# Moving the sums and squares of two layer norms from VectorE's batch statistics to ScalarE's accumulator output

## The reference

```
def _ln(x, w, b, eps=1e-05):
    m = x.mean(-1, keepdims=True)
    v = ((x - m) ** 2).mean(-1, keepdims=True)
    return (x - m) / jnp.sqrt(v + eps) * w + b
...
xa = _ln(x, ln1_w, ln1_b)            # "recurrent" norm, on the MLP's result
... token shift, mixes, projections, decay w, scan s = a + w * s, group norm og ...
x1 = x + og * g @ Wo.T
xc = _ln(x1, ln2_w, ln2_b)           # "channel" norm, on the recurrent part's result
sx2 = jnp.concatenate([state[:, 0:1] - xc[:, :1], xc[:, :-1] - xc[:, 1:]], axis=1)
rr = jax.nn.sigmoid((xc + sx2 * ffn_maa_r) @ Wfr.T)
kk = jnp.square(jax.nn.relu((xc + sx2 * ffn_maa_k) @ Wfk.T))
return x1 + rr * (kk @ Wfv.T)
```

## Time and profile before

| | |
|---|---|
| three timed runs | 1116.63, 1121.56, 1121.56 us, median 1121.56 |
| profiled execution | 1118.86 us, of which the span of the trace is 1117.1 |
| busy over the span | PE 1061.3 us (95%), DVE 916.1 (82%), ACT 702.6 (63%), POOL 608.1 (54%) |
| steady steps | from about 540 to 910 us |
| steps with the first channel runs, then the list behind step 15 | from about 936 and about 1020 us |
| granted TensorE clock | 0.989 of full speed |

### The profile page before, as it was taken

The page is one execution under the profiler, slowest core; times in us unless marked ns, Lnnn a source line. Parts: engine busy times, 40 slices in busy tenths (PEclk is TensorE's granted clock), DMA queues, the critical chain, the costliest instruction groups (busy, mean ns, idle before and its releaser), DMA issues.

```text
span 1117.1 us, 34410 instructions
## 1 busy us (share of the span) xinstructions
PE 1061.3 (95%) x12992; PEld 883.5 (79%) x12992; DVE 916.1 (82%) x1662; ACT 702.6 (63%) x1606; POOL 608.1 (54%) x535
## 2 busy tenths in 40 slices
PE   5999999999999998999999999999999998788898
PEld 4888988888889887777787877777777776566687
DVE  5997777888777776228999999999999999999753
ACT  5678878777777775465556555456555455544574
POOL 4787887877887885024443454443454443444233
PEclk9999999999999998999999999999999999998999
DMA  8500000011111110013333331233331233304011
GB/s 328 174 4 2 0 0 2 3 41 41 41 48 38 38 47 3 1 28 68 79 83 86 85 70 40 64 81 84 84 76 40 56 82 86 85 10 114 20 38 57
DMA packets 39867, 65.01 MB, mean 58 GB/s; under 512 B 4384, under 2 KB 26208, under 8 KB 39392
## 3 DMA queue, kind: packets, MB, share of 16 engines
q1 hardware_dynamic: 39776, 63.75, 21.4%
HBM read 55.35 MB, written 8.39 MB: 57 GB/s over the span
## 4 chain that ended last, share of the span: by engine, by line
PE 60%; DVE 27%; issue 7%; ACT 3%; DVEq 1%; DMA 1%; SPq 0%; POOL 0%; ACTq 0%; POOLq 0%
PE psum L353 9%; DVE shared L1788 9%; PE psum L267 5%; PE psum L999 5%; PE psum L336 5%; PE psum L1008 4%; PE psum L368 4%; PE psum L1089 4%; DVE shared L1774 4%; PE psum L297 4%; PE psum L280 3%; DVE late_mixed L1754 3%; PE psum L1270 2%; PE psum L310 2%; PE psum L1300 2%
## 5 line engine op out<-in xcount | busy, mean ns | idle before, releaser
L1788 DVE TENSOR_TENSOR_SCAN shared<-late_wT,shared 128x512 f32<-128x512 f32 x128 | 192.4, 1503 | 0.0
L232 POOL TENSOR_TENSOR shared<-shared,att_row_max 128x512 f32<-128x512 f32 x128 | 132.3, 1051 | 17.9 <-DVE att_row_max L564 17.9
L353 PE MATMUL psum<-shared 128*128 128x128 f32 x1024 | 126.6, 277 | 0.0
L453 ACT ACTIVATE shared<-shared 128x512 f32<-128x512 f32 x128 | 80.5, 631 | 67.7 <-POOL shared L232 67.6
L353 PEld LDWEIGHTS psum<-shared 128*128 128x128 f32 x1024 | 121.0, 194 | 0.3 <-ACT shared L462 0.2
L999 PE MATMUL psum<-late_glnT,w 128*128 128x256 f32 x512 | 119.5, 387 | 1.8 <-ACT late_glnT L1378 1.8
L1008 PE MATMUL psum<-w,late_hT 128*128 128x256 f32 x512 | 120.0, 383 | 1.0 <-ACT late_hT L1387 0.9
L564 DVE TENSOR_REDUCE att_row_max<-shared 128x8 f32<-128x512 f32 x128 | 86.9, 680 | 40.9 <-POOL shared L225 40.9
L903 POOL TENSOR_TENSOR shared<-shared,late_rT 128x512 f32<-128x512 f32 x32 | 40.7, 1273 | 140.6 <-DVE shared L1788 140.6
L894 POOL TENSOR_TENSOR late_xm<-late_mixed,late_xa 128x512 f32<-128x512 f32 x64 | 79.7, 1255 | 59.9 <-DVE late_mixed L1754 56.3
L999 PEld LDWEIGHTS psum<-late_glnT,w 128*128 128x128 f32 x512 | 95.8, 192 | 17.9 <-issue 2.8
(11 more groups left out here) (168 smaller groups left out, 2420.9 us busy)
## 6 DMA issues: line engine op xcount, KB each, us to landing
shared<-v_rows SPq DMA_DIRECT2D x64, 512.0 KB, 7.1
shared<-in_enc SPq DMA_DIRECT2D x64, 128.0 KB, 2.6
v_rows<-shared SPq DMA_DIRECT2D x64, 64.0 KB, 1.8
out<-x SPq DMA_DIRECT2D x16, 256.0 KB, 2.0
x<-in_x SPq DMA_DIRECT2D x7, 512.0 KB, 9.7
w<-in_w SPq DMA_DIRECT2D x2, 1024.0 KB, 16.9
shared<-in_cross_mask SPq DMA_DIRECT2D x1, 1024.0 KB, 11.4
shared<-in_w_qkv SPq DMA_DIRECT2D x1, 768.0 KB, 4.5
```

Source lines behind the costliest of these rows:

```text
L232: nc.gpsimd.tensor_tensor(zs, zs, peak.unsqueeze(2).to_broadcast([P, PAIRS, S]), ALU.subtract).then_inc(shifted, 1)
L353: last = nc.tensor.matmul(dst[:, half * P:(half + 1) * P], w[:, kb, c0 + half * P:c0 + (half + 1) * P], src[:, u % 2, kb, 0:P], start=(kb ...
L453: nc.scalar.activation(probs[:, u % 2, half * 4:(half + 1) * 4, :].rearrange("p r k -> p (r k)"), z[:, u % 2, half, :], ACT.Exp).then_inc( ...
L1788: nc.vector.tensor_tensor_scan(states, wT[:, u, half, :, :, :].rearrange("p j b t -> p (j b t)"), states, 0.0, ALU.mult, ALU.add).then_inc ...
```

## The change

The statistics of both norms go to ACT. For a run, `mlp_moments` is now: two Copy activations of the tile whose accumulator output is the row sum (the copied tile goes to `xn`, used as scratch), two small activations that scale the sums to -mean and to a shift, and two Square activations whose bias is the shift and whose accumulator output is the variance. `make_stats` is the same with one small activation, split in two functions, `out_means` and `out_variances`. DVE loses L1721 to L1731, L1857 and all of `ch_variances`; `ch_invert` reads the variances directly, and `ch_shifts` the sums.

```diff
+            def mlp_moments(g):
+                act.wait_ge(mlp_x, g + 1)
+                if later(g):
+                    act.wait_ge(xnT_ready, g)
+                act.nop(nofuse=True)
+                for c in range(CH):
+                    last = nc.scalar.activation(xn[:, c, :], core.x[:, ds(g * CH + c, C)], ACT.Copy,
+                                                accum_out=mlp_sum[:, c:c + 1])
+                last.then_inc(mlp_sum_ready, 1)
+                act.wait_ge(mlp_sum_ready, g + 1)
+                nc.scalar.activation(mlp_shift[:, :], mlp_sum[:, :], ACT.Copy, scale=-(C ** -1.5)).then_inc(mlp_mean_ready, 1)
+                nc.scalar.activation(neg_mean[:, :], mlp_sum[:, :], ACT.Copy, scale=-1.0 / C).then_inc(mlp_mean_ready, 1)
+                act.wait_ge(mlp_mean_ready, 2 * g + 2)
+                act.nop(nofuse=True)
+                for c in range(CH):
+                    last = nc.scalar.activation(xn[:, c, :], core.x[:, ds(g * CH + c, C)], ACT.Square, scale=C ** -0.5,
+                                                bias=mlp_shift[:, c:c + 1], accum_out=moments[:, CH + c:CH + c + 1])
+                last.then_inc(moments_ready, 1)
+            def out_means(r):
+                act.wait_ge(x_ready, r + 1)
+                act.wait_ge(xnT_ready, runs_by(r + 4))
...
+                nc.scalar.activation(out_shift[:, :], ch_mean[:, ds(r, CH)], ACT.Copy,
+                                     scale=-(C ** -1.5)).then_inc(out_mean_ready, 1)
+            def out_variances(r):
...
             def ch_invert(i):
-                act.wait_ge(norm_var, i + 1)
+                act.wait_ge(stats_ready, NORMS[i][1])
...
-                    for q in range(UPS):
-                        gelu(s + 3, q)
+                    gelu(s + 3, 0)
+                    gelu(s + 3, 1)
+                if there(s + 2):
+                    mlp_moments(s + 2)
+                if there(s + 3):
+                    gelu(s + 3, 2)
+                    gelu(s + 3, 3)
...
+                if there(s - 2) and not s_is(s, RUNS - 1):
+                    out_means(s - 2)
                 if there(s - 1) and not s_is(s, RUNS - 1):
                     square(s - 1)
...
+                if there(s - 2) and not s_is(s, RUNS - 1):
+                    out_variances(s - 2)
                 if not s_is(s, RUNS - 1):
                     nc.scalar.preload_act_table_set("natural_log_exp_and_others")
...
             ch_square(EARLY + 1, 1)
+            make_stats(RUNS - 3)
             square(RUNS - 1)
...
             ch_tanh(EARLY + 3, 1)
+            make_stats(RUNS - 2)
             channel(EARLY + 3, 1)
             ch_copy_in(EARLY + 6, 0)
+            make_stats(RUNS - 1)
             nc.scalar.preload_act_table_set("natural_log_exp_and_others")
             ch_invert(2)
```

More of the change, by code:

```diff
@@ new lines, in out_means @@
+            def out_means(r):
+                act.wait_ge(x_ready, r + 1)
+                act.wait_ge(xnT_ready, runs_by(r + 4))
+                act.nop(nofuse=True)
+                for c in range(CH):
+                    t = r * CH + c
+                    last = nc.scalar.activation(xn[:, c, :], core.x[:, ds(t, C)], ACT.Copy, accum_out=ch_mean[:, ds(t, 1)])
+                last.then_inc(out_sum_ready, 1)
+                act.wait_ge(out_sum_ready, r + 1)
+                act.nop(nofuse=True)
+                nc.scalar.activation(out_shift[:, :], ch_mean[:, ds(r, CH)], ACT.Copy,
+                                     scale=-(C ** -1.5)).then_inc(out_mean_ready, 1)
@@ new lines, in out_variances, with make_stats @@
+            def out_variances(r):
+                act.wait_ge(out_mean_ready, r + 1)
+                act.nop(nofuse=True)
+                for c in range(CH):
+                    t = r * CH + c
+                    nc.scalar.activation(xn[:, c, :], core.x[:, ds(t, C)], ACT.Square, scale=C ** -0.5,
+                                         bias=out_shift[:, c:c + 1], accum_out=ch_var[:, ds(t, 1)]).then_inc(stats_ready, 1)
+            def make_stats(r):
+                out_means(r)
+                out_variances(r)
@@ L1507, in ch_invert @@
                 part = slice(*NORMS[i])
-                act.wait_ge(norm_var, i + 1)
+                act.wait_ge(stats_ready, NORMS[i][1])
                 act.wait_ge(gxn_ready, RUNS)
-                nc.scalar.activation(core.norm_tmp[:, 0, part], core.norm_tmp[:, 2, part], ACT.Ln,
+                nc.scalar.activation(core.norm_tmp[:, 0, part], ch_var[:, part], ACT.Ln,
                                      bias=core.eps[:, :]).then_inc(norm_logged, 1)
@@ L1716, in mlp_residual @@
                 nc.vector.tensor_tensor(xs, mlp, xs, ALU.add).then_inc(mlp_x, 1)
-            def mlp_moments(g):
-                dve.wait_ge(mlp_x, g + 1)
-                for c in range(CH):
-                    last = nc.vector.bn_stats(run_stats[:, c, :], core.x[:, ds(g * CH + c, C)])
-                last.then_inc(run_stats_ready, 1)
-                dve.wait_ge(run_stats_ready, 2 * g + 1)
-                if later(g):
-                    dve.wait_ge(shift_ready, g)
-                dve.nop(nofuse=True)
-                for c in range(CH):
-                    last = nc.vector.bn_aggr(moments[:, c:c + CH + 1:CH], run_stats[:, c, :])
-                last.then_inc(run_stats_ready, 1)
-                dve.wait_ge(run_stats_ready, 2 * g + 2)
-                nc.vector.tensor_scalar(neg_mean[:, :], moments[:, 0:CH], -1.0, None, ALU.mult).then_inc(moments_ready, 1)
             def mixer_input(r):
@@ L1945, in body @@
                             ch_mix(early_run(s, 0), 0)
-                        if there(s + 2) and not s_is(s, -2):
-                            mlp_moments(s + 2)
                         if there(s - 2) and not early(s):
@@ L1952, in body @@
                         mix(s + 1, 1)
-                    if n == 3 and there(s - 2) and not s_is(s, RUNS - 1):
-                        make_stats(s - 2)
-                    if s_is(s, RUNS - 4) and n == 4:
-                        ch_variances(0)
                     if n == 4:
@@ L1981, in _ @@
             attention_residual(1, end)
-            mlp_moments(0)
             spreads(att.first_mlp)
@@ L1988, in _ @@
             add_heads(RUNS - 1, 1)
-            make_stats(RUNS - 3)
             sum_squares(RUNS - 2)
-            ch_variances(1)
             ch_mix(EARLY + 1, 1)
@@ L2001, in _ @@
             add_residual(RUNS - 2)
-            make_stats(RUNS - 2)
             ch_mix(EARLY + 4, 0)
@@ L2006, in _ @@
             add_residual(RUNS - 1)
-            make_stats(RUNS - 1)
-            ch_variances(2)
             ch_mix(EARLY + 5, 1)
```

40 lines of the change are left out of this document (11 added, 29 removed).

## The result

The changed kernel takes 1113.11 us (median of four runs, 1112.77 to 1115.22) beside 1121.1 of the kernel before; the recorded ratio of the runs is 0.9945, with a 95% interval from 0.9928 to 0.9962 (the two medians alone would give 0.9929). Run once more among later kernels it took 1115.20 (six runs), ratio 0.9953 [0.9936, 0.9969]. It is faster by about half a per cent, where I had forecast 1122 and no change. Its profiled execution took 1112.93 us with a span of 1111.1.

The account below looks back on a forecast made before the run. PE's own work was taken as the bound, 33.44 us a period, with DVE 0.07 above. Terms 0.6 + 1.3 - 1.4 - 1.4 - 0.7 - 1.5 + 2.8 + 2.8 = +2.5 us on 1119.6 gave 1122 us, range 1115.5 to 1129.5.

Parts of the forecast that it names:

- PE's own work is a floor of 33.44 us: Steady period: PE's work alone takes 33.44 us, DVE stands 0.07 above, so DVE's relief gives at most 0.07.
- +0.6: Steady steps 2 to 11: ACT's later `decay` starts the fifth mix 0.06 us later in each, +0.6 us.
- DVE would wait ahead of the fifth mix: Steady period: DVE, arriving 2.0 us earlier, waits at the fifth mix for `decay_expd`, so ACT's `decay` sets the period.
- The start: Step -2: `mlp_moments` at 3.05 us delays the gelus, and PE's `down` waits for the last one: +1.3 us.
- Step 12: Step 12: `ch_variances(0)` on DVE had pushed the mixes back; without it, -1.4 us.
- Step 13: Step 13: DVE reaches `ch_finish` 2.0 us earlier, but ACT can take the keys only some 1.4 earlier: -1.4 us.
- Step 14: Step 14: loses only DVE's statistics, -0.7 us.
- The list: Work behind the last step: less DVE work before the mixes -1.5 us; `make_stats(13)` and `make_stats(15)` in ACT's chain +2.8 each.
- r: What writing out the accumulator adds to an ACT activation: taken as 0.2 us, between nothing and 0.29.
- PE has room: Rival: matmuls close up once DVE is early, periods shrink towards 31.5 us, up to 20 us gained, 1100; chance 0.06.
- ACT sets the pace: Rival, slower: costlier accumulator writes or waits on ACT; +5.4 us at 0.29 a write, +9 (1128) at 0.4; chance 0.27.
- Only the end is faster: Rival: ACT's blocks at 1056 and 1084 hide, sum -3.1 us, 1119; chance 0.17 shared with a free accumulator.

Follow-up runs that it names:

- e1: Changed kernel with DVE also redoing its old batch statistics in the steps and at the start, into an unread scratch tile; 1120.94 us, ratio 1.0009.
- e2: Changed kernel with the two squares of `out_variances` done twice in each step, the extra pair into scratch; 1126.81 us, ratio 1.0078.
- e4: Kernel before with only `mlp_moments` moved to ACT, channel norms' statistics left on DVE; 1114.58 us, ratio 0.9955.
- e5: Kernel before with only the channel norms' statistics moved to ACT, `mlp_moments` left on DVE; 1117.25 us, ratio 0.9985.
- e11: Changed kernel run and traced once more, unaltered; 1115.20 us, ratio 0.9953.
- e12: Changed kernel with six unread matmuls in PE's wait ahead of the last block; 1115.04 us, ratio 0.9958.
- e2b: e2 with no accumulator output on the extra pair of squares; 1121.76 us, one run.
- e3: Changed kernel with the channel norms' last group of statistics, in the list at the end, given back to DVE; 1110.94 us, ratio 0.9925.
- e6: Changed kernel with `make_stats(13)` one place later in ACT's list and the statistics of `make_stats(15)` back on DVE; 1110.48 us, ratio 0.9916.
- e13: e6 with four unread matmuls in PE's wait ahead of `project_out(14)`; 1109.05 us, ratio 0.9904.
- e8: Changed kernel with ten unread matmuls in PE's wait ahead of the last block; 1116.47 us, ratio 0.9961.
- e9: Changed kernel with `make_stats(13)` moved as in e7, eight unread matmuls ahead of `project_out(15)` and ten ahead of the last block; 1115.85 us, ratio 0.9968.
- e7: Changed kernel with `make_stats(13)` one place later in ACT's list, behind a `ch_tanh`; 1113.10 us, ratio 0.9947.

## Why the prediction was wrong

**The step that failed is "PE's own work is a floor of 33.44 us ... Relief of DVE can give at most 0.07 us a period there".** The 33.44 us were not PE's own work. They held 0.17 us of waiting for DVE's last read of the states ahead of WrT (1.90 in place of 1.73 at 633.50), and the other periods up to 0.36; without it PE needs 33.24 us. The one period I read was also the shortest of the nine (33.43 to 33.60 us between L1026's starts). The chain laid it to PE, since the gap before the row is short (0.13 us at 700.48) and the rest of it stretches the row itself from 1.89 to 1.99. The wait of PEld in the earlier trace rows was that very wait, 0.4 us in each period, of which 0.27 reached the matmuls; I called it hidden "for the most part by the matmuls ahead" and didn't compare the row with others of its kind. With DVE's work gone the term is -2.78 and not +0.6; with it put back (e1) it is -0.57.

**That DVE would wait ahead of the fifth mix** was wrong: with the time it no longer loses it comes to the first mix before PE is ready, and waits there. Counted from where PE starts its `up` product of the period, before and after,

```profile
676.75 3.72 PE L999 MATMUL psum<-late_glnT,w 128*128 128x256 f32 x16
```

```profile
674.71 3.72 PE L1001 MATMUL psum<-late_glnT,w 128*128 128x256 f32 x16
```

ACT's copy of V comes at 13.52 us in both kernels (690.27 and 688.23). `decay` ends at 17.35 us (692.06) where it had ended at 17.11 (693.86): later by 0.24 and not by the 0.69 of the prediction, since `out_variances` takes 689.92 - 688.83 = 1.09 us where I had 1.41. The fifth mix then starts at 17.48 us, 0.31 earlier than before (694.54). The place was right all the same: one more microsecond there and ACT does set the pace (e2). The slack is 0.1 us.

**The start** was mis-sized: +1.3, measured +0.29. Of the difference 0.84 is `mlp_moments`, which moved the queue by 469.44 - 467.23 (the end of the second gelu pair) = 2.21 us where I had taken 3.05, and 0.14 that the last two gelu pairs ran without a gap (1.54 and not 2 x 0.84). e4 and e5 show that the 0.3 is `mlp_moments`'.

**Step 12** was right, -1.4 and -1.49, and for the reason given (e1 and e4 against e5). **Step 13**, -1.4 against -2.20: I let ACT's later work keep 0.6 of DVE's 2.0, and it kept nothing; PE's wait for `ch_finish` fell from 2.92 to 1.25 us. **Step 14**, -0.7 against -0.96, is right: with VectorE's statistics put back (e1) it is 35.58 us, in e4, where they never left VectorE, 35.65, and before 35.59, while e11 has 34.61 and the changed kernel 34.63.

**The list.** The -1.5 before the mixes was -2.2: from the account's -8.63 at the end of step 14 to 1042.42 - 1053.27 = -10.85 at the key product behind the mixes. From there to `project_out(14)` (1067.56 before, 1058.11 after) 1.40 us came back. That is `make_stats(13)`, in ACT's chain as said, for 2.3 us where I had 2.8, less 0.87 by which the product at 1053.27 was slower in the trace of before (2.88 us in its chain, 2.01 after). `make_stats(15)` was +2.8 against +3.48: ACT's part is 2.3, and 1.2 is TensorE at its lower clock behind the longer wait, a term that I didn't have (e12, and e2, e2b and e5, whose traces had the full clock there).

**r** was 0.095 and not 0.2, inside the bounds. By the prediction's own terms that alone would have made the sum about 0: the periods on its floor (-0.6), the start +0.9, the two blocks of the list 2.4 each. It would still have been "the same", so r wasn't the error. The rest was shorter than reckoned as well: ACT's three pieces cost 2.21 + (686.54 - 685.43 = 1.11) + 1.09 = 4.4 us a period and not 5.9.

**The rivals.** *PE has room* was the true one, with its size wrong by far: matmuls "that look back to back" did close up, by 0.27 us a period and not by 2. The Trainium skill, "Perfetto Trace Analysis", Identifying the Most-Contended Engine, says that the busy share of matmuls doesn't tell how near PE is to its limit; I had dismissed it. The rows agree with it now: PE was busy 33.50 of 33.50 us before and after. The busy share of the weight loads, which the same section would look at beside the MFU, hardly tells the two apart either (26.37 us before, 26.45 after); it was the wait of PEld that pointed at the 0.27. *ACT sets the pace* falls for this kernel and holds for e2. *Only the end is faster* falls: the end costs 2.7 us net, and e3, e6 and e13 win it back.

**What stays open.** By the two traces the change is worth 5.97 - 1.49 = 4.5 us behind the start, by e11's in place of the first 2.2 (1117.1 - 462.39 against 1113.8 - 461.33); by the times it is 5.9 (1119.92 against 1114.07, the median of its ten runs). All have the clock in them and the times the start as well, each worth some 2 us from one execution to the next, and of the kernel before there is one trace alone, so I can't divide the difference between them. Why PE's first instructions behind a wait are slow in one execution and not in the next stays open too.

## What to carry to other kernels

A chain that runs on one engine alone is no proof of that engine's floor: compare each row in it with others of its shape, and a short wait of the weight loads that comes in every period is a wait of the path until shown otherwise. Where another engine stands within some tenths of the bound, price its relief from such rows; half of this change (e4) gives all of the steady gain, and the other half, by the changed kernel beside e4, brings 0.9 us in step 12, 1.0 in step 14 and the cost at the end. Work moved onto an engine costs nothing in a loop where it idles (here with 0.1 us to spare) and its full length in a tail where it leads, so move it there by its place and not by its kind.

## What the runs showed of the hardware

- The accumulator output of an activation is an instruction of its own, ACTIVATION_READ_ACCUMULATOR, 187 to 197 ns long, which lies over its neighbours and costs the queue 0.095 us (e2 against e2b).
- Behind a wait of 1.5 to 2.9 us the first one to three groups of PE instructions ran at the lower of its two clocks in some executions and not in others: 3.56 to 3.65 us for a product of 1.97 in step 13 of five traces (e1, e4, e5, e8, e9), with the clock granted at 0.51 to 0.53; 2.40 to 3.35 for `project_out(14)` in eight (e1, e2b, e3, e5, e6, e7, e8, e11), where it took 1.99 in the changed kernel's and five more. The Trainium skill, "TensorE: Matmul & The Clock Gate", Part 1, says of the slow matmuls at a kernel's start that their number varies from run to run of the same kernel; behind a wait the changed kernel's two traces agree (1.99 and 2.74 us for the same piece). Behind a wait filled with matmuls that nobody reads the clock was full in all six cases (four ahead of the last block, two ahead of `project_out(14)`); it was full behind nine of the twenty-one bare waits at these places too.
- With the clock full, the steady part (L1028's starts in steps -1 and 12) is 425.62 and 425.63 us in the changed kernel's two traces, and 425.62 to 425.66 in the nine other kernels with the same steps, so a period's difference of 0.02 us can be read from one trace, while the time of the kernel before varied by 6.5 us.
